# 4,096-key cross-attention on one Trainium2 core: maxima as four array quarters beside the masks, four score banks, three banks for maxima

## The reference

```
scores = q @ k.T * scale ; masked keys get a very large negative number
p = exp(scores - rowmax(scores))        # 256 x 4096
out = (p @ v) / rowsum(p)
```

## Time and profile before

| | |
|---|---|
| three runs | 984.84, 994.50, 998.21 us; median 994.5 |
| the profiled execution | 993.12 us, span of its instructions 991.4 us |
| granted TensorE clock, mean over the span | 0.99 |
| busy: PE, PEld, DVE, ACT | 945.7, 556.7, 595.1, 455.2 us |

### The profile page before, as it was taken

How to read it: one execution, slowest core, us unless ns; L and a number is a source line. 1 busy time by engine, 2 the same in 40 slices (tenths; PEclk the granted TensorE clock), 3 DMA queues, 4 the chain that set the end, 5 groups by cost and what they waited for, 6 DMA issues and landing times.

```text
span 991.4 us, 20180 instructions
## 1 busy us (share of the span) xinstructions
PE 945.7 (95%) x7230; PEld 556.7 (56%) x7230; DVE 595.1 (60%) x1543; ACT 455.2 (46%) x848; POOL 99.5 (10%) x135
## 2 busy tenths in 40 slices
PE   5999999999899999889999999999999999977998
PEld 5888885565466666644444444444444444456656
DVE  2455354653222212777777777777777777658883
ACT  3444434531021122566666666666666666642102
POOL 1223330002401011100000000000000000001000
PEclk9999999999899999999999999999999999999999
DMA  7744699116104733794554455544555444710000
GB/s 260 259 164 162 233 345 362 67 46 235 38 27 74 107 117 96 174 279 65 80 78 70 63 68 79 76 64 63 73 79 76 62 58 100 129 44 1 1 1 22
DMA packets 77731, 108.94 MB, mean 110 GB/s; under 512 B 27593, under 2 KB 63789, under 8 KB 73648
## 3 DMA queue, kind: packets, MB, share of 16 engines
q1 hardware_dynamic: 72376, 92.45, 42.8%
q0 software_dynamic: 5104, 15.36, 4.2%
q10 hardware_dynamic: 200, 0.44, 0.2%
HBM read 84.61 MB, written 21.82 MB: 107 GB/s over the span
## 4 chain that ended last, share of the span: by engine, by line
PE 83%; DVE 7%; DMA 3%; SPq 3%; issue 2%; ACT 1%; another core or an unknown queue 0%; POOL 0%; ACTq 0%; DVEq 0%
PE bank L1415 14%; PE bank L1436 13%; PE bank L1424 9%; PE bank L1282 8%; PE bank L1393 7%; PE bank L1085 5%; PE bank L1306 4%; PE bank L1072 4%; PE bank L1643 2%; PE bank L1447 2%; PE bank L1255 2%; PE bank L1167 1%; PE bank L1705 1%; PE bank L1176 1%; SPq L468 1%
## 5 line engine op out<-in xcount | busy, mean ns | idle before, releaser
L934 ACT ACTIVATE region<-bank 128x512 f32<-128x512 f32 x512 | 277.9, 595 | 156.5 <-PE bank L1424 156.5
L2076 DVE CUSTOM_DVE_ANT_0 xnT<-bank,region 128x1024 bf16<-128x1024 f32 x128 | 156.1, 1219 | 84.5 <-issue 84.5
L1415 PE MATMUL bank<-region 128*128 (+1 forms) x1024 | 157.1, 275 | 2.3 <-ACT region L934 1.8
L2076 DVE CUSTOM_DVE_ANT_0 region<-bank,region 128x1024 bf16<-128x1024 f32 x128 | 156.3, 1221 | 0.9 <-issue 0.5
L1436 PE MATMUL bank<-region 128*32 128x256 f32 x2048 | 138.9, 385 | 0.0
L1415 PEld LDWEIGHTS bank<-region 128*128 128x128 bf16 x1024 | 69.2, 97 | 119.5 <-issue 59.8
L1424 PE MATMUL bank<-region,identb 64*64 64x512 bf16 x1024 | 105.0, 400 | 0.0
L1436 PEld LDWEIGHTS bank<-region 128*32 128x32 f32 x2048 | 58.8, 109 | 34.3 <-ACT region L934 14.5
L1393 PE MATMUL bank<-region,xnT 64*128 64x512 bf16 x248 | 74.9, 382 | 1.6 <-DVE region L2076 1.1
L1282 PE MATMUL bank<-region 128*128 x240 | 75.2, 467 | 1.2 <-DVE region L1989 1.2
L1395 PE MATMUL bank<-region,xnT 64*128 64x512 bf16 x248 | 74.9, 382 | 0.0
(11 more groups left out here) (349 smaller groups left out, 1169.5 us busy)
## 6 DMA issues: line engine op xcount, KB each, us to landing
region<-keys_split SPq DMA_DIRECT2D x224, 128.0 KB, 5.0
region<-in_ctx SPq DMA_DIRECT2D x32, 512.0 KB, 6.4
keys_split<-region POOLq DMA_DIRECT2D x48, 256.0 KB, 4.3
region<-in_L_ffn_we_gate SPq DMA_DIRECT2D x8, 688.0 KB, 9.3
region<-in_L_ffn_we_up SPq DMA_DIRECT2D x8, 688.0 KB, 10.6
region<-in_L_ffn_we_down SPq DMA_DIRECT2D x8, 640.0 KB, 9.9
region<-in_mask_1x1xSxS_ik SPq DMA_DIRECT2D x1, 4096.0 KB, 17.0
mask_kept<-region SPq DMA_DIRECT2D x1, 2048.0 KB, 10.4
```

The source lines that it names most:

```text
L934: nc.scalar.activation(prob4[n % PROBS].rearrange("p a b -> p (a b)"), bank[:, SCORE4[n], :], ACT.Exp, scale=SCALE4).then_inc(exp4_ready, 1)
L1415: mm(bank[:, SCORE4[n], k * S:(k + 1) * S], slab[s][:, t * P:(t + 1) * P], qT4[:, bass.ds(u, 1), :].rearrange("p o q -> p (o q)"), start=( ...
L2076: v.tensor_tensor_reduce(out=junk[q], in0=bank[:, 3 + 2 * q:5 + 2 * q, :].rearrange("p a b -> p (a b)"), in1=maskN[:, q, 2 * c * CH:2 * (c ...
```

## The change

- `max_pair` for units 1 to 31 issues four matmuls on 64x64 quarters (64 rows of contraction, 64 queries, 512 keys) in place of two on 64x128 halves, and signals once for the pair in place of twice. Unit 0 is as before.
- Its two banks come from `MAX4`, which uses banks 3, 4 and 5 only. The wait (`max_banks_free`) is now for all takes before the pair but the last.
- VectorE takes each bank by itself, 128x512, so two takes a pair, each with its own piece in `cmax` and its own signal. The memset stays one a pair.
- Scores use banks 0, 1, 2 and 6 in turn (`score_bank`); the last unit keeps the old order of banks.
- The order on TensorE: each group is followed by one pair, directly behind its mask; the wait for the pair's banks stands between the two halves of the group's scores. `sum_rows` stands between scores and mask of group 3.
- Before the first unit only pair 0 of unit 1 is computed; pair 1 comes in the first group of unit 0.

```diff
--- before.py
+++ after.py
@@ -67,12 +67,24 @@
 NEG_ROWS = slice(32, 34)
 GROUPS = 8
 HALVES = 2 * GROUPS
-SCORE4 = (0, 1, 2, 0, 1, 2, 0, 1, 0, 2, 1, 0, 2, 1, 0, 2)
+SCORE4 = (0, 1, 2, 6) * (HALVES // 4)
+LAST_SCORE4 = (0, 1, 2, 0, 1, 2, 0, 1, 0, 2, 1, 0, 2, 1, 0, 2)
 NEG4 = 1
 KT4 = CTX // P
 RING = 4
 MAXES = GROUPS
-LAST_USE4 = [max(m for m in range(n - HALVES, n) if SCORE4[m % HALVES] == SCORE4[n]) for n in range(HALVES)]
+MAX4 = ((3, 4), (5, 3), (4, 5), (3, 4), (3, 5), (4, 3), (5, 4), (3, 5))
+
+
+def score_bank(u, n):
+    return (LAST_SCORE4 if isinstance(u, int) and u == U4 - 1 else SCORE4)[n]
+
+
+def last_use(u, n):
+    banks = SCORE4 + tuple(score_bank(u, m) for m in range(n))
+    return max(m - HALVES for m, b in enumerate(banks) if b == score_bank(u, n))
+
+
 AHEAD = 2
 PAIRS = GROUPS // 2
 PROBS = 8
@@ -312,7 +324,7 @@
         pv_sb = [A1.take([S + QT * (DH4 + 1)]) for s in range(2)]
         bo4 = A1.take([D])
         A1 = Arena(region, A1.at + 1024, total)
-        cmax = [A1.take([QT, GROUPS // 2]) for s in range(2)]
+        cmax = [A1.take([QT, GROUPS]) for s in range(2)]
         negmax = A1.take([2, QT])
         negparts = A1.take([QT, 4], BF16)
         orec = A1.take([QT])
@@ -931,7 +943,7 @@
                     if n == 14 and last:
                         squares(0)
                     act.wait_ge(score4, HALVES * u + n + 1)
-                    nc.scalar.activation(prob4[n % PROBS].rearrange("p a b -> p (a b)"), bank[:, SCORE4[n], :],
+                    nc.scalar.activation(prob4[n % PROBS].rearrange("p a b -> p (a b)"), bank[:, score_bank(u, n), :],
                                          ACT.Exp, scale=SCALE4).then_inc(exp4_ready, 1)
             for s in range(RING):
                 softmax_numerators(s, s, s == 0)
@@ -1377,29 +1389,36 @@
                                                q_rows[:, t, half_h * 8 + h, :], identb[:, :])
                 last.then_inc(qT_psum, 1)
 
+            def max_banks_free(u, m):
+
+                if not isinstance(u, int) or u > 0:
+                    pe.wait_ge(max_taken, 2 * (u * MAXES + m) - MAXES - 1)
+                elif m >= 2:
+                    pe.wait_ge(max_taken, m - 1)
+
             def max_pair(s, u, m):
 
                 q, c = m % 2, 2 * (m // 2)
                 b = 3 + 2 * (m % 2)
-                k = u * MAXES + m
-                if not isinstance(k, int) or k >= 2:
-                    pe.wait_ge(max_taken, k - 1)
                 if isinstance(u, int) and u == 0:
                     mine = qT4[:, 0, q * P:(q + 1) * P]
                     mm(bank[:, b, :], mine, slab[s][:, c * CH:(c + 1) * CH], start=True, stop=True)
                     mm(bank[:, b + 1, :], mine, slab[s][:, (c + 1) * CH:(c + 2) * CH], start=True, stop=True)\
                         .then_inc(max_psum, 1)
                 else:
-                    mm(bank[:, b, :], qmax4[s][0:64, q * P:(q + 1) * P], slab[s][0:64, c * CH:(c + 1) * CH], start=True, stop=True)\
-                        .then_inc(max_psum, 1)
-                    mm(bank[:, b + 1, :], qmax4[s][64:P, q * P:(q + 1) * P], slab[s][64:P, (c + 1) * CH:(c + 2) * CH],
-                       start=True, stop=True).then_inc(max_psum, 1)
+                    for h in range(2):
+                        for r in range(2):
+                            i, o = slice(64 * r, 64 * r + 64), 64 * (r ^ h)
+                            last = mm(bank[o:o + 64, MAX4[m][r], :], qmax4[s][i, q * P + o:q * P + o + 64],
+                                      slab[s][i, (c + r) * CH:(c + r + 1) * CH],
+                                      start=True, stop=True, skip_group_check=True)
+                    last.then_inc(max_psum, 1)
 
             def negmax_T(u):
 
                 pe.wait_ge(negmax_ready, u + 1)
                 if not isinstance(u, int) or u > 0:
-                    pe.wait_ge(exp4_ready, HALVES * u + LAST_USE4[NEG4] + 1)
+                    pe.wait_ge(exp4_ready, HALVES * u + last_use(u, NEG4) + 1)
                 for q in range(QT):
                     last = nc.tensor.transpose(bf16_bank(SCORE4[NEG4])[NEG_ROWS, q * P:(q + 1) * P], negparts[:, q, 0:2],
                                                identb[:, :])
@@ -1407,21 +1426,21 @@
 
             def score_half(s, u, n):
 
-                done = HALVES * u + LAST_USE4[n] + 1
+                done = HALVES * u + last_use(u, n) + 1
                 if not isinstance(done, int) or done > 0:
                     pe.wait_ge(exp4_ready, done)
                 for k in range(2):
                     t = 2 * n + k
-                    mm(bank[:, SCORE4[n], k * S:(k + 1) * S], slab[s][:, t * P:(t + 1) * P],
+                    mm(bank[:, score_bank(u, n), k * S:(k + 1) * S], slab[s][:, t * P:(t + 1) * P],
                        qT4[:, bass.ds(u, 1), :].rearrange("p o q -> p (o q)"),
                        start=(k == 0), stop=False, skip_group_check=True)
 
-            def score_mask(g):
+            def score_mask(u, g):
 
                 for k in range(2):
                     for r in range(2):
                         i, o = slice(64 * r, 64 * r + 64), slice(64 * (r ^ k), 64 * (r ^ k) + 64)
-                        last = mm(bank[o, SCORE4[2 * g + k], :], identb[i, i],
+                        last = mm(bank[o, score_bank(u, 2 * g + k), :], identb[i, i],
                                   maskT[i, 4 * g + 2 * k:4 * g + 2 * k + 2, :].rearrange("p a b -> p (a b)"),
                                   start=False, stop=True, skip_group_check=True)
                     last.then_inc(score4, 1)
@@ -1456,32 +1475,35 @@
                 def slab_there(r):
                     pe.wait_ge(slab_loaded[r], (fills + (1 if r < s else 0)) * 16 * SLAB_LOADS - (48 if r == 0 else 0))
 
-                def maxima(m):
-                    if m < MAXES:
-                        if left >= 1:
-                            max_pair(s1, u + 1, m)
-                    elif left >= 2:
-                        max_pair(s2, u + 2, m - MAXES)
-
                 def score_group(g):
-                    for n in (2 * g, 2 * g + 1):
-                        score_half(s, u, n)
-                    score_mask(g)
+
+                    m = AHEAD + g
+                    s_m, u_m, n_m = (s1, u + 1, m) if m < MAXES else (s2, u + 2, m - MAXES)
+                    wanted = left >= (1 if m < MAXES else 2)
+                    score_half(s, u, 2 * g)
+                    if wanted and not (first and g == 0):
+                        if m == MAXES:
+                            slab_there(s2)
+                        max_banks_free(u_m, n_m)
+                    score_half(s, u, 2 * g + 1)
+                    if g == 3 and not first:
+                        sum_rows(s - 1, u - 1)
+                    score_mask(u, g)
+                    if first and g == 0:
+                        max_banks_free(u_m, n_m - 1)
+                        max_pair(s_m, u_m, n_m - 1)
+                        max_banks_free(u_m, n_m)
+                    if wanted:
+                        max_pair(s_m, u_m, n_m)
 
                 pe.wait_ge(negT_ready, u + 1)
                 for j in range(PAIRS):
                     score_group(2 * j)
-                    if left >= 2 and AHEAD + 2 * j == MAXES:
-                        slab_there(s2)
-                    maxima(AHEAD + 2 * j)
-                    maxima(AHEAD + 2 * j + 1)
                     if between is not None:
                         between(j, False)
                     score_group(2 * j + 1)
                     if j == PAIRS - 1 and left >= 1:
                         negmax_T(u + 1)
-                    if j == 1 and not first:
-                        sum_rows(s - 1, u - 1)
                     for g in (2 * j - 2, 2 * j - 1):
                         if j > 0:
                             values_group(s, u, g)
@@ -1554,6 +1576,7 @@
             between4 = {1: 2, 2: 3, 5: 4, 6: 5}
             for m in range(MAXES):
                 pe.wait_ge(qT_ready, min(m + 1, QT))
+                max_banks_free(0, m)
                 max_pair(0, 0, m)
                 if m in between4:
                     queries_T(between4[m])
@@ -1561,10 +1584,10 @@
                     spin(2, 2)
             queries_T(6)
             queries_T(7)
+            pe.wait_ge(slab_loaded[1], 16 * SLAB_LOADS)
+            max_banks_free(1, 0)
             spin(2, 4)
-            pe.wait_ge(slab_loaded[1], 16 * SLAB_LOADS)
-            for m in range(AHEAD):
-                max_pair(1, 1, m)
+            max_pair(1, 1, 0)
             pe.wait_ge(qT_ready, 2 * TT)
             negmax_T(0)
             pe.wait_ge(v_blank, 2)
@@ -2071,17 +2094,26 @@
 
                 k = u * MAXES + m
                 q, c = m % 2, m // 2
-                dve.wait_ge(max_psum, 2 * k + 2 - MAXES if not isinstance(k, int) or k >= MAXES else k + 1)
+                dve.wait_ge(max_psum, k + 1)
                 v.memset(small[0:1, 4 + q:5 + q], 0.0)
```

(21 more changed lines are left out.)

## The result

The changed kernel takes 1079.9 us (median of 4 runs) against 996.4 for the kernel before in the same measurement: ratio 1.085, 95% interval 1.077 to 1.092. Three of the four runs took 1066.2, 1079.3 and 1080.5 us; the fourth took 1258.9 at a granted clock of 0.74, where the others had 0.98 and 0.99, and is left out of the ratio. The prediction was 1070 us, range 1037 to 1095. The profiled execution took 1079.3 us, its span is 1077.4.

The account below looks back on a forecast made before the run. The prediction took TensorE's sum of work to bound the attention loop; 993.1 us plus 84.9 and 9.3 of stalls, minus 14.9 for shapes and 1.5 for row sums, gave 1070.9, stated as 1070 us, range 1037 to 1095.

Parts of the forecast that it names:

- The wait for pair k - 1: Between an odd group's score halves, TensorE must wait for the first take of the pair just before: 123 stalls.
- Its size: Stall ahead of the third score in odd groups: 0.69 us each, 123 times, 84.9 us.
- TensorE woken by such a take, 0.06: Last step of the odd-group stall: TensorE's matmul starts 0.06 us after the take ends.
- The start of a unit: Stall after group 7's pair, where VectorE copies the transposed maxima before the take: 0.31 us, 30 times, 9.3 us.
- Changes of shape: Mask to maxima takes 0.22 us instead of 0.34 with equal 64x64 shapes: 0.12 a turn, 14.9 us gained.
- Row sums: Moved to between scores and mask, they save one change of shape: 0.05 us a unit, 1.5 us gained.
- The fourth score bank at nothing: In the loop, a fourth score bank gains 0, as TensorE loses nothing there to waits for ScalarE.
- the sum of 77.8: Total predicted slowdown: 84.9 plus 9.3 us of stalls, minus 14.9 for shapes and 1.5 for row sums.
- Rival 2: Quarters of the maxima run two by two, each pair 0.43 us instead of 0.22: about 1124 us, chance 5%.
- rival 3: VectorE's sum of work becomes the bound, with takes of 0.94 us: about 1101 us, chance 5%.
- Rival 1: Ahead of the odd score half the take is not waited for: 977 us, down to 962, chance 7%.
- decides from 0.53 us: No odd-group stall if first take plus hand-over end under 0.53 us after the even group's maxima start.

Follow-up runs that it names:

- e4: Changed kernel, TensorE's program written out, wait for the maxima's banks moved behind the mask, directly ahead of the maxima: 986.0 us, 0.995 of the kernel before.
- e7: e3 with takes of 256 of each bank's 512 columns, half the keys left out of the maxima: 1031.8 us, 1.035 of the kernel before.
- e11: Kernel before with only the row sums moved, to between scores and mask of group 3: 982.5 us, 0.991 of the kernel before.
- e2: Kernel before, TensorE's program written out for units 4 to 27, maxima there as four 64x64 quarters: 1.003 of the kernel before.
- e10: Changed kernel's order and quarters with the kernel before's three score and four maxima banks, 1,024-column takes and row sums' place: 1019.9 us, 1.026 of the kernel before.
- e12: Changed kernel with the dummy matmuls put back ahead of the wait for the second slab of keys: 1076.3 us, 1.080 of the kernel before.
- e3: Changed kernel with TensorE's program written out in place of its hardware loop: 1.073 of the kernel before.
- e5: e4 with the maxima of even groups moved ahead of their mask: 982.3 us, 0.985 of the kernel before.
- e6: e5 with the dummy matmuls put back ahead of the wait for the second slab of keys: 0.987 of the kernel before.

## Why the prediction was right

- **The wait for pair k - 1.** Right in place, kind and number. e4 and e7 show it from two sides: move the wait and the loss is gone, shorten the take and the stall shrinks by the same.
- **Its size.** 0.69 stood between what the written-out units and group 1 show (0.66) and the other groups of the loop (0.73). The step that was a little off is "TensorE woken by such a take, 0.06": it holds for the first kind, the others have 0.13 to 0.15. VectorE starts 0.44 after the maxima and not 0.47, which takes back 0.03 in both. The take itself is 687 ns, as worked out from the rows of 344 and 1,024 columns. The Trainium skill, "VectorE: DVE Perf Modes", section on the TRN2 errata, has beside the figure quoted in the prediction also (columns + 151) / 0.96 for a float32 `tensor_tensor`. That estimate is 691 ns for 512 columns and 424 for 256; the runs show 687 (the changed kernel) and 419 (e7), so this form fits the take, though the Trainium skill gives it for another operation; its form for a PSUM source (an estimate of 658) doesn't.
- **The start of a unit.** Forecast 0.31, measured 0.30 to 0.41 in the hardware loop and about 0.19 in the written-out units: 9.8 us where 9.3 was forecast.
- **Changes of shape.** Forecast 0.12 a turn, measured 0.10: mask to maxima is 0.24, not 0.22, and maxima to scores 0.32, not 0.31.
- **Row sums.** The weakest term: 0.05 a unit forecast, 0.19 measured here and 0.19 in e11. I had kept nearly all of the 0.55 as the sums' own loads; part of them runs ahead under the scores, and one change of shape is gone; how the 0.19 splits between the two is open.
- **The fourth score bank at nothing.** Right against the kernel before, where TensorE waits for ScalarE in the first and last units only, but the prediction didn't weigh how close that was: in before ScalarE was just in time, as e2 shows, and in the new order three score banks would have cost 0.32 in each odd group (e10).
- **Missed:** the profiled execution is 86.2 us over before's, 8.4 more than the sum of 77.8. 2.8 us of that come from the clock and the DMAs before any changed code, in this execution and not in each: in e12 the wait for that slab ends at 429.3, in e3 at 427.8, in before at 428.9. 1.0 us is the move of the dummy matmuls, which I did not price. About 4 us are the low clock at the loop's start; what brought it is not shown, since e3 has the same move and only a short low stretch. 0.4 us lie behind the loop.
- **Where luck helped.** The terms of the loop that were priced come out at 77.9 against 77.8, because their errors cancel: +1.3 for the stalls and +0.5 at the start of a unit, +2.5 for the smaller gain on the changes of shape, -4.2 for the row sums. The mechanism does not hang on that, since e4 and e7 show the stall, by far the largest term, by itself.
- Rival 2 is out by e2, rival 3 by e4 and e7. Rival 1's "decides from 0.53 us" is what e4 and e5 used: not a faster take, but more work ahead of the wait.

## What to carry to other kernels

When a buffer is taken away, write down for each wait how old the work is that it waits for, in microseconds of the waiting engine's own work, and compare that with the reader's latency from start to signal; busy shares say nothing about it. Put such a wait as far behind independent work as its use allows. And when an edit saves time on the bounding engine, look at which neighbour was only just in time (here ScalarE, which by e2 had next to nothing to spare), since it takes the gain back until it, too, gets a buffer.

## What the runs showed of the hardware

- Four 64x64 quarters with different weights ran in one pass beside each other, and their weight loads ran under the mask matmuls on the same quarters (641.19 under 641.17): 0.24 from one set of four to the next, 0.31 to 0.34 to another array shape.
- A take split in two costs VectorE little: the second half follows after 0.62 us, so two are 1.30 us against 1.22 for one of double width.
- Single executions of one kernel differ by some 15 us with the granted clock: the kernel before took 984.9 us at 0.995 and 999.6 at 0.978 in one measurement. The profile of the changed kernel has a stretch of 20.5 us at 1.2 GHz from 160 us on, long before the changed code, and TensorE was busy in all of the 8 us ahead of it; before has 2.4 GHz there. Unit lengths from the profile repeat to 0.02 us (13.48 in e5 and e6, 16.44 and 16.43 in the changed kernel and e12) and told the experiments apart where medians could not.
